# Moving the store of x1 behind the row of maxima in a gated cross-attention and feed-forward block

## The reference, cut to what matters

```
x1  = x + tanh(g_xattn) * MHA(layernorm(x), ctx, ctx)     # q from x, k and v from ctx, softmax over 256 keys
f   = fake_quant(layernorm(x1), clip_x)                   # scale from the maximum over the WHOLE tensor
h   = fake_quant(silu(f @ Wg.T) * (f @ Wu.T), clip_down)  # again one scale for the whole tensor
out = x1 + tanh(g_ffn) * (h @ Wd.T)
```

## Time and profile before

| | us |
|---|---|
| time of 3 runs: median, lowest, highest | 1844.71, 1842.28, 1851.07 |
| profiled execution, its own time | 1839.49 |
| its span, first to last instruction | 1837.7 |
| PE busy in the span | 1634.8 (89%) |
| DVE busy | 1288.7 (70%) |
| ACT busy | 846.9 (46%) |
| POOL busy | 517.8 (28%) |
| attention bodies (112 to 1204 of the span), PE busy | 1035.05 of 1092.00 |
| share of q1, SP's queue, in the DMA engines' time | 59.5% |
| mean granted TensorE clock | 0.953 |

### The profile page before, as it was taken

The page is one execution under the profiler, slowest core; times in us unless marked ns, Lnnn a source line. Parts: engine busy times, 40 slices in busy tenths (PEclk is TensorE's granted clock), DMA queues, the critical chain, the costliest instruction groups (busy, mean ns, idle before and its releaser), DMA issues.

```text
span 1837.7 us, 33988 instructions
## 1 busy us (share of the span) xinstructions
PE 1634.8 (89%) x11880; PEld 769.5 (42%) x11880; DVE 1288.7 (70%) x2055; ACT 846.9 (46%) x1132; POOL 517.8 (28%) x782
## 2 busy tenths in 40 slices
PE   3859999899999999999999999946699999989887
PEld 2324444444444444444454444423344444434333
DVE  6727677776776777777767767657787778778555
ACT  3223534435335244253353352426777777755242
POOL 6114324234134243242341432202000000007644
PEclk7979999999999999999999999987799999989999
DMA  6649567577486586675865954543145543016897
GB/s 189 166 137 180 127 162 175 145 174 158 138 186 137 152 186 152 169 161 144 190 142 134 196 137 116 127 166 125 37 180 219 202 171 132 23 47 259 338 419 297
DMA packets 274971, 307.57 MB, mean 167 GB/s; under 512 B 152112, under 2 KB 201264, under 8 KB 272304
## 3 DMA queue, kind: packets, MB, share of 16 engines
q1 hardware_dynamic: 274864, 306.00, 59.5%
HBM read 176.17 MB, written 95.94 MB: 148 GB/s over the span
## 4 chain that ended last, share of the span: by engine, by line
PE 50%; issue 25%; DMA 9%; DVE 8%; POOL 3%; SPq 2%; ACT 2%; DVEq 0%; POOLq 0%; ACTq 0%
PE bank L1322 12%; PE bank L1223 10%; PE bank L1225 10%; PE bank L1224 10%; PE spair L1304 5%; DMA x<-out_dram 4%; DMA stacks<-mT 4%; POOL yh L625 3%; PE spair L1279 2%; DVE mx L917 2%; ACT pr L668 1%; DVE ndev L960 1%; DMA hb<-in_L_ffn_w_gate_dram 1%; PE bank L1214 1%; DVE xres L937 1%
## 5 line engine op out<-in xcount | busy, mean ns | idle before, releaser
L668 ACT ACTIVATE pr<-spair 128x1024 f32<-128x1024 f32 x256 | 259.3, 1020 | 182.4 <-PE spair L1304 182.4
L917 DVE TENSOR_REDUCE mx<-spair 128x4 f32<-128x1024 f32 x256 | 301.5, 1219 | 57.4 <-PE spair L1279 56.9
L895 DVE SCALAR_TENSOR_TENSOR parts<-bank,bqk,parts 128x512 f16<-128x512 f32 x128 | 96.1, 751 | 241.5 <-ACT parts L657 235.9
L1304 PE MATMUL spair<-stacks 128*128 128x256 f16 x1024 | 161.3, 287 | 53.5 <-DMA stacks<-mT 44.2
L1420 PE MATMUL spair<-xqT,wgT 128*128 128x512 bf16 x704 | 182.5, 382 | 1.2 <-ACT xqT L781 1.2
L1420 PE MATMUL spair<-xqT,wuT 128*128 128x512 bf16 x704 | 182.1, 381 | 0.0
L657 ACT ACTIVATE parts<-bank,bqk 128x512 f16<-128x512 f32 x128 | 88.0, 687 | 172.4 <-PE bank L1225 172.3
L1322 PE MATMUL bank<-pr,v 128*32 128x256 f32 x2048 | 143.1, 399 | 27.0 <-DVE o L911 25.2
L764 ACT ACTIVATE sil<-spair,gsc 128x512 f32<-128x512 f32 x176 | 118.2, 680 | 75.6 <-PE spair L1420 75.5
L1304 PEld LDWEIGHTS spair<-stacks 128*128 128x128 f16 x1024 | 91.6, 101 | 143.7 <-DMA stacks<-mT 51.8
L535 POOL TENSOR_TENSOR cl<-cbuf,ch 128x512 f16<-128x512 f32 x64 | 77.0, 1207 | 259.1 <-ACT ch L645 258.9
(11 more groups left out here) (172 smaller groups left out, 3273.7 us busy)
## 6 DMA issues: line engine op xcount, KB each, us to landing
stacks<-qk_spill SPq DMA_DIRECT2D x384, 128.0 KB, 4.2
qk_spill<-parts SPq DMA_DIRECT2D x64, 512.0 KB, 3.0
x<-out_dram SPq DMA_DIRECT2D x32, 1024.0 KB, 11.0
h_spill<-hb SPq DMA_DIRECT2D x10, 2816.0 KB, 9.2
hb<-h_spill SPq DMA_DIRECT2D x10, 2816.0 KB, 15.3
xbuf<-in_x_dram SPq DMA_DIRECT2D x16, 1024.0 KB, 6.9
cbuf<-in_ctx_dram SPq DMA_DIRECT2D x16, 1024.0 KB, 6.6
xres<-in_x_dram SPq DMA_DIRECT2D x16, 1024.0 KB, 5.6
```

What stands on the lines that cost most here:

```text
L668: act.activation(pr[:, u % 4, :, :, :].rearrange("p a b q -> p (a b q)"), spair[u % 2][:, :, :].rearrange("p a q -> p (a q)"), ACT.Exp, sc ...
L895: dve.scalar_tensor_tensor(out=parts[:, c, 2 * w + 1, :], in0=pj[(g + 1) % 3][:, :], scalar=bqk[:, w, c:c + 1], in1=parts[:, c, 2 * w, :], ...
L917: dve.tensor_reduce(mx[:, h:h + 2, b, :], spair[u % 2][:, :, :].rearrange("p a (q k) -> p a q k", q=KH), AX_X, ALU.max).then_inc(max_done, 1)
L1304: last = pe.matmul(spair[u % 2][:, a, kh * S:kh * S + S], kst[:, h, b * S + kh * P:b * S + kh * P + P], qst[:, h, b * S:b * S + S], start= ...
```

## The change

Two calls of `store_x1` move on SP. In a body the store of group j is no longer the last step. The next body issues it as its second step, behind its row of maxima. The one that was the last step of the last body now stands behind the final `mrow` and ahead of `load_res`. Which bytes are moved, the number of transfers and all semaphores stay; the other engines' instructions stay too.

```
             def body(i, j, par, more, first=False):
                 mrow(j)
+                if not first:
+                    store_x1(j - 1)
                 spill(i, 0)
                 spill(i, 1)
                 if not first:
...
                 if more > 1:
                     load_x(i + 2)
-                store_x1(j)
 
             body(1, 0, 1, 2, first=True)
             body(2, 1, 0, 2)
...
             mrow(NG - 1)
+            store_x1(NG - 2)
             load_res(NG - 1)
```

## The result

| | before | changed |
|---|---|---|
| time, median (lowest to highest) | 1845.13 us (1842.28 to 1851.07) | 1795.74 us (1794.6 to 1801.7) |
| ratio, 95% interval | | 0.9735 (0.9703 to 0.9767) |
| the profiled execution's own time | 1839.49 us | 1795.86 us |

The kernel is 2.7% faster. The direction and the mechanism were forecast. The time lies 9 us under the forecast and 1.3 us under the low end of the range. The saving between the medians is 49.4 us, between the two profiled executions 43.6 us; 39.9 us were forecast for both.

A forecast was written before the change was run, and what follows sets the result against it. TensorE, busy 89% of the span, was taken to bound the kernel, idling at seams for the row of maxima. Savings of 34.4 + 2.5 + 3 = 39.9 us gave a forecast of 1805 us, range 1797 to 1823.

The forecast's parts named there:

- What the row waited for: At the seams between bodies: the row of maxima's landing is set by the 1 MB store ahead, not its own issue.
- The row alone, 2.1 us: The row of maxima with no store ahead lands about 2.1 us from issue, between 1.7 and 4.1.
- What the seam gives, 34.4 us: TensorE's idle 2.48 us go nearly whole at 14 seams: 36.5 us of wait less 2.1 us, giving 34.4 us.
- the last row, 2.5 us: In the last body, where TensorE waits 5.01 us, the score starts at 1206.65 instead of 1209.14: 2.5 us saved.
- the row's scatter: Allowance of 0.15 us at each of 14 seams for variation in the row's landing, 2.1 us in all.
- What was called covered: The moved store, SP's later spill and load, and GpSimd's root of x1 were to cost nothing at the seams.
- The clock, 3 us: Fewer falls to half clock behind the attention stage's seams were to save 3 us, from 0 to 5.4.
- I count half of it: Half of 5.4 us for nine falls counted, 3 us, since short gaps among scores and exponentials stay.
- the price is read from mT to mT ... 0.6 us: One clock fall's price from two bodies: 72.65 us with it, 72.05 without, so 0.6 us, or 5.4 for nine.
- the same 40 us off: The saving reckoned on the profiled 1839.5 us was taken off the runs' median of 1844.7 us, giving 1804.8.

The follow-up runs named there:

- filled kernel: Against the kernel before, in its order: ten 512-column products put on TensorE in the idle gap at 14 seams; 1831.93 us against 1847.96 us, ratio 0.9914.

## Why the prediction was right and where it failed

**What the row waited for: right.** "The row's landing is set by the 1 MB ahead of it in the queue" holds for a read as for a store, and a quarter of it ahead delays the row far less.

**The row alone, 2.1 us: right to the tenth.** The sum of a start, the bytes and the acknowledgement, read off a spill, gave it. By the Trainium skill (page "DMA: Bandwidth & Descriptors", section "Anatomy of one DMA") the estimate was 2.04 us; the trace agrees with 2.1.

**What the seam gives, 34.4 us, and the last row, 2.5 us: right.** The filled kernel isolates both as 36.6 us against 36.9, and its 14 bodies as 34.1 us against 34.4. Against the first profile itself the wait shrank by 36.0 us. The 0.15 us a seam that I took off "for the row's scatter" is near the truth by luck: what lies between 36.0 and 34.1 is not scatter of the new row, but two old rows that an instruction transfer had made late. Whether the last row's 2.5 us reach the end is open.

**What was called covered: right.** The store's landing, SP's list and GpSimd's root cost nothing: the bodies take 69.6 us, where "about 70" was forecast. But VectorE does come ahead of the root, which I had behind it, and waits 0.63 us. The cover behind it held.

**The clock, 3 us: wrong, and this is the failed step.** Between medians it measured 16.0 us, with up to 2 us of shorter waits in it; in single profiles the clock cost 7.3, 9.4 and 15.0 us. Two things went wrong in it. First, "I count half of it": I allowed that the short gaps behind the seam hold the clock down too. They don't, since with the long gap filled or gone the mean over the 14 bodies is 1.00. Second, "the price is read from mT to mT ... 0.6 us": one pair of bodies, and a cheap one. The nine falls of that same profile cost 0.5 to 1.3 us each, 7.3 us and not 5.4. In others some falls last longer and cost 2.0 us.

**From one execution to the median: wrong by the same cause.** I took "the same 40 us off" the median, though the profiled execution was 5.2 us quicker than it. I treated that difference as if both kernels had it. But before scatters by 17 us and the changed kernel by 8, so part of what made the execution quick is something that the change removes. Between the profiles 43.6 us were saved, between the medians 49.4 and 52.6. The recorded clocks of the executions point to the same cause: of 62 of the kernel before, the nine that took less than 1842 us were granted 0.957 on average over the whole span, the eight over 1850 us 0.950. The longer falls found in the execution of 1849.88 us are of the size of the difference; only three executions were profiled, so how many falls each has is not shown. With the clock at 16 instead of 3 the sum would have been 53 us and 1792 us forecast, against 1795.7 measured; the range's low end, which took 5.4 us as the most that the clock could give, is where it had to break.

## What to carry to other kernels

When a few bytes on the critical path share a queue with a bulk transfer, issue them first: here they waited for what had been issued ahead of them, even on another queue. Look for TensorE gaps that recur and ask for the clock behind them; here gaps of 2.3 us and more had a fall behind most of them, and two gaps of 1.1 and 1.2 us too. The price of a fall is not in the gap. Here it was 16 us beside 36.5 us of gaps, and it is best read by filling the gap with idle work in the kernel as it is, not from one pair of bodies. Where a kernel's runs scatter and the profiled one lies off the median, find out what scatters before taking a saving over to the median.

## What the runs showed of the hardware

- An idle gap of 2.3 to 3.6 us at every seam: TensorE's clock was at half behind 9 of 14 seams in the first profile (mean 0.98) and for longer in another (0.97). Gaps of 4.5 to 4.9 us gave a mean of 0.96 over their bodies. With gaps of 0.2 to 1.3 us it was 1.00 in one kernel, and in another it fell behind two of the five seams whose gaps were 1.1 to 1.6 us.
- A fall can cost 0.6 or 2.0 us in neighbouring bodies with the same instructions.
- A 16 KB transfer behind 1 MB on another queue, issued 0.88 us later, landed no earlier than behind it on one queue (4.6 us from the first issue); issued in the same moment it was 1.3 us late; issued 0.38 us ahead it wasn't touched.
- Where a transfer of the instruction queue q8 fell into the seam, the row of maxima was late: with the score 5.83 and 5.38 us behind mT instead of 4.7 in the kernel before, and 2.48 and 2.40 instead of 2.1 to 2.3 in the changed one.
